# A transformer block with a mixture of experts: the experts' weights applied by one broadcast product on GpSimd instead of four multiplications on ScalarE

## The reference

```python
g_idx = argmax(g_logits)                        # one of 2 groups per token
topv, topi = top_k(softmax(e_sel), 2)           # 2 of the group's 4 experts
topv = topv / (topv.sum(-1) + 1e-8)
comb = zeros((S, 8)).at[rows, g_idx*4 + topi].add(topv)
h_expert = swiglu(flat @ expert_in_w.T)
for e in range(8):
    routed += comb[:, e:e+1] * (h_expert @ expert_out_weight[e].T)
out = out_shared + routed
```

## Time and profile before

| | |
|---|---|
| median of 3 runs | 1200.93 us (1200.56 to 1201.93) |
| span of the profiled execution, first to last instruction | 1198.4 us |
| time of the profiled execution with what lies around the span | not given by itself; median less span is 2.5 us |
| TensorE busy | 1062.6 us (89%) |
| VectorE busy | 760.6 us (63%) |
| ScalarE busy | 629.2 us (52%) |
| GpSimd busy | 388.1 us (32%) |
| mean granted TensorE clock | 0.939 of full speed |

### The profile page before, as it was taken

One profiled execution on the slowest core, in us unless ns is written; L12 is line 12 of the kernel. 1 busy time (PEld: TensorE's weight loads), 2 busy tenths in 40 slices (PEclk: granted clock), 3 DMA queues, 4 the chain that ended last, 5 costly groups with the idle time before them and its releaser, 6 DMA issues.

```text
span 1198.4 us, 20365 instructions
## 1 busy us (share of the span) xinstructions
PE 1062.6 (89%) x5632; PEld 707.3 (59%) x5632; DVE 760.6 (63%) x2118; ACT 629.2 (52%) x1395; POOL 388.1 (32%) x514
## 2 busy tenths in 40 slices
PE   2579988999799988899888998889989899899997
PEld 1345566556675566655666556755567455675575
DVE  3378547873768547686486854777467763778444
ACT  1226825567345745467344672546734576456744
POOL 5411424314341234313352142431433213341133
PEclk9969989999898998899889998989988999899999
DMA  3430033004040040400413003310314004040000
GB/s 94 71 40 2 14 41 59 19 2 54 10 59 10 1 53 10 67 1 1 53 26 50 1 11 42 55 22 1 41 12 66 13 2 53 10 63 1 1 2 18
DMA packets 28540, 34.39 MB, mean 29 GB/s; under 512 B 5402, under 2 KB 15552, under 8 KB 28336
## 3 DMA queue, kind: packets, MB, share of 16 engines
q1 hardware_dynamic: 28464, 33.55, 18.2%
HBM read 3.61 MB, written 4.19 MB: 7 GB/s over the span
## 4 chain that ended last, share of the span: by engine, by line
PE 62%; issue 11%; DVE 8%; DMA 6%; POOL 5%; SPq 4%; ACT 3%; DVEq 0%; POOLq 0%; ACTq 0%
PE bank L523 12%; PE pair L494 10%; PE bank L542 9%; PE bank L494 5%; DMA k_stack<-qk_h 5%; SPq L367 4%; PE pair L662 4%; PE pair L663 4%; PE pair L664 4%; PE bank L643 2%; ACT pt L975 2%; PE pair L425 1%; PE pair L426 1%; PE pair L427 1%; PE bank L644 1%
## 5 line engine op out<-in xcount | busy, mean ns | idle before, releaser
L975 ACT ACTIVATE pt<-bank 128x512 f32<-128x512 f32 (+3 forms) x768 | 348.6, 494 | 230.8 <-PE bank L523 223.6
L747 DVE CUSTOM_DVE_ANT_0 pair<-pair,causal 128x640 f32<-128x640 f32 (+3 forms) x256 | 258.8, 1046 | 59.3 <-PE pair L494 44.8
L523 PE MATMUL bank<-q_stack,k_stack 128*128 128x512 f32 (+2 forms) x768 | 268.9, 402 | 7.8 <-ACT pt L975 6.3
L523 PEld LDWEIGHTS bank<-q_stack,k_stack 128*128 128x128 f32 x768 | 137.9, 193 | 160.2 <-ACT pt L975 127.6
L1119 POOL TENSOR_SCALAR_AFFINE_SELECT pt<-pt 128x512 f32<-128x512 f32 x128 | 81.6, 638 | 391.9 <-ACT pt L975 391.9
L494 PE MATMUL pair<-k_stack,q_stack 112*128 112x512 f32 (+2 forms) x512 | 156.2, 396 | 22.6 <-DVE mx L747 12.3
L747 DVE CUSTOM_DVE_ANT_0 bank<-bank,causal 128x128 f32<-128x128 f32 (+3 forms) x256 | 122.6, 507 | 73.3 <-PE bank L494 73.1
L542 PE MATMUL bank<-pt,v 128*32 128x512 f32 (+3 forms) x1536 | 165.5, 503 | 2.2 <-POOL pt L1119 1.8
L494 PEld LDWEIGHTS pair<-k_stack,q_stack 112*128 112x128 f32 x512 | 90.9, 202 | 62.4 <-DVE mx L747 42.3
L494 PE MATMUL bank<-k_stack,q_stack 112*128 112x256 f32 (+2 forms) x256 | 90.0, 424 | 33.2 <-DMA k_stack<-qk_h 23.8
L662 PE MATMUL pair<-wex_h,hid_h 128*128 128x512 f32 x256 | 106.3, 415 | 0.7 <-POOL hid_l L1142 0.4
(11 more groups left out here) (142 smaller groups left out, 1528.7 us busy)
## 6 DMA issues: line engine op xcount, KB each, us to landing
q_stack<-qk_h SPq DMA_DIRECT2D x64, 128.0 KB, 4.1
k_stack<-qk_h SPq DMA_DIRECT2D x64, 128.0 KB, 6.2
q_stack<-qk_l SPq DMA_DIRECT2D x32, 128.0 KB, 5.0
k_stack<-qk_l SPq DMA_DIRECT2D x32, 128.0 KB, 6.7
out<-h SPq DMA_DIRECT2D x16, 256.0 KB, 2.3
pt<-w_expert SPq DMA_DIRECT2D x1, 1024.0 KB
x_sb<-x_t SPq DMA_DIRECT2D x8, 116.0 KB
pos_sb<-pos SPq DMA_DIRECT2D x1, 512.0 KB
```

Of the source, the lines that this page charges most:

```text
L523: nc.tensor.matmul((b4, b5)[p % 2][:, c0:HALF], k_stack[:, hd // 2, kt * P:(kt + 1) * P], q_stack[:, half, hd, c0:HALF], start=True, stop= ...
L747: nc.vector.tensor_tensor_reduce(src, src, causal[:, S - n:S], 1.0, -3.0e38, ALU.add, ALU.max, mx[:, col:col + 1]).then_inc(s_taken, 1)
L975: nc.scalar.activation(pt[:, k % PT_SLOTS, j, q0:HALF], (b4, b5)[p % 2][:, q0:HALF], ACT.Exp, scale=0.25).then_inc(exp_done, 1)
```

## The change

The four multiplications on ScalarE and their semaphore go. GpSimd waits for VectorE's `sel_made` itself and makes all four products with one `tensor_tensor` of 4 x 128 columns, in which `wsel` is broadcast along the 128 columns; it counts as a fourth step of `ex_step`, so every wait on `ex_step` counts by 4 per tile. The three additions stay.

```diff
-COMBINE = 3
+COMBINE = 4
...
-                elif kind == "combine":
-                    t = st[1]
-                    act.wait_ge(sel_made, i * TILES + t + 1)
-                    for e in range(EG):
-                        part = slice(e * P, (e + 1) * P)
-                        nc.scalar.mul(from_act[:, t % 2, part], from_dve[:, t % 2, part],
-                                      wsel[:, t, e:e + 1]).then_inc(weighted, 1)
...
-                pool.wait_ge(weighted, (i * TILES + t + 1) * EG)
+                pool.wait_ge(sel_made, i * TILES + t + 1)
+                nc.gpsimd.tensor_tensor(four.rearrange("p (e c) -> p e c", c=P),
+                                        from_dve[:, slot, :].rearrange("p (e c) -> p e c", c=P),
+                                        wsel[:, t, :].unsqueeze(2).to_broadcast([P, EG, P]),
+                                        ALU.mult).then_inc(ex_step, 1)
+                pool.wait_ge(ex_step, done + 1)
                 nc.gpsimd.tensor_tensor(two, four[:, 0:2 * P], four[:, 2 * P:4 * P], ALU.add).then_inc(ex_step, 1)
                 if t % HT == 0:
                     pool.wait_ge(base_made, i * 2 + t // HT + 1)
-                pool.wait_ge(ex_step, done + 1)
+                pool.wait_ge(ex_step, done + 2)
                 nc.gpsimd.tensor_tensor(acc[:, t, :], acc[:, t, :], two[:, 0:P], ALU.add).then_inc(ex_step, 1)
-                pool.wait_ge(ex_step, done + 2)
+                pool.wait_ge(ex_step, done + 3)
                 nc.gpsimd.tensor_tensor(acc[:, t, :], acc[:, t, :], two[:, P:2 * P], ALU.add).then_inc(ex_step, 1)
```

More of the change, by code:

```diff
@@ L300, in build @@
         shared_ready, base_made = sem("shared_ready"), sem("base_made")
-        ex_ready, sela_made, sel_made, weighted, ex_step = (
-            sem(n) for n in ("ex_ready", "sela_made", "sel_made", "weighted", "ex_step"))
+        ex_ready, sela_made, sel_made, ex_step = (sem(n) for n in ("ex_ready", "sela_made", "sel_made", "ex_step"))
         out_done = [sem(f"out_done_{half}") for half in range(2)]
@@ L1042, in stage @@
                     front(i, st[0], st[1])
-                elif st[0] in ("in", "counts", "expert", "combine"):
+                elif st[0] in ("in", "counts", "expert"):
                     forward(i, st)
```

## The result

The kernel with the change takes 1222.43 us (median of 4 runs, 1221.86 to 1225.06), the one before 1200.74 us (4 runs, 1200.00 to 1201.93): 1.0183 times as long, 95% interval 1.0169 to 1.0197.

A forecast was written before the change was run, and what follows sets the result against it. The prediction took the kernel as bound by TensorE and its waits, chiefly for VectorE's z. It summed 7 x 2.4 = 16.8, image 7 +1.7 and clock +1.4 to 19.9 us, giving 1220.5 us, range 1207 to 1230.

The forecast's parts named there:

- likeliest case: Whole kernel: products on GpSimd hold VectorE one instruction each; 1220.5 us, own range 1216 to 1225, chance 0.52.
- Removed products: ScalarE's 256 products, 81.7 us, go; what is queued behind them waits for other engines, so gain on the path 0.
- Price of the product: GpSimd's new 128x512 product taken at 1.29 us from the nearest row; a combine becomes 1.37 us longer.
- One VectorE instruction per GpSimd instruction: VectorE instructions with two SBUF inputs, and its z, are held; about one gets through per wide GpSimd instruction.
- The stage: Combines 2 and 3 of a steady image: routing and next z held, last z 2.4 us later, combine 1's 0.2 included.
- combine 1: Steady image: the combine ends at 605.0, not 604.18, and overlaps z2, which passes +0.2 us to TensorE's transposes.
- Combine 0 and combines 4 to 7: Rest of a steady image: products take as long as before, are hidden or end in time; cost 0.
- Image 7: Last image: product meets the routing, +0.4 us, and GpSimd runs without rest at the end, +1.3 us; 1.7 together.
- Clock: TensorE after the z stall: a longer stall makes the slow stretch more common, +0.2 us per image, 1.4 us.
- milder holding: Rival: only the instruction that meets a product waits longer, 1.4 us per image; 1212 us, chance 0.25.
- freed ScalarE: Rival: L899 of tile 1 waited for L1021 behind ScalarE's products, up to 1.27 us per image gained; 1191 us, chance 0.03.
- missing hold: Rival: no hold for a product reading few distinct weights, or VectorE wins the race; only the end longer, 1202 us, chance 0.08.

The follow-up runs named there:

- the kernel with six tiles on GpSimd: The changed kernel, but tiles 2 and 3 of each image keep ScalarE's four products: 1200.14 us, ratio 1.0010 to the kernel before.
- the gate: GpSimd starts combine 2 only when the next image's last z is made: 1193.29 us added to the kernel before, 1211.40 us added to the changed kernel.
- the changed kernel with the wait: The changed kernel, with GpSimd's combine 2 held back until the next image's last z is made: 1211.40 us, ratio 1.0073 to the kernel before.
- the eleven unused matmuls: Kernel before, combine 2 waiting for the last z, 5 unused matmuls in TensorE's stall, 11 more at an image's start: 1189.96 us, ratio 0.9938.
- the kernel before with the same wait: The kernel before, with GpSimd's combine 2 held back until the next image's last z is made: 1193.29 us, ratio 0.9941.

## Why the prediction was right

1220.5 us was forecast and 1222.43 measured, in the likeliest case's own range. The accounting below is of the profiled 21.7 us: TensorE's waits for z +12.0 and z2 +1.3; its smaller waits for VectorE +1.2 (L493 for mx 8.5 to 9.5, for from_dve 4.6 to 5.5, and so on, by the lists of both kernels); the same matmuls at a lower clock +6.0; from the last matmul to the last GpSimd start 4.59 us, before 4.11, +0.5. That is 21.0, of which 15.0 are the waits and the longer end; 0.7 us are not placed.

- **Removed products: gain 0.** Right. Loading ScalarE again changed nothing that can be measured; leaving the product out altogether gained 0.13%, which bounds what any freed engine could give.
- **Price of the product.** 1.29 us was taken, and "nothing suggests less" was wrong: 1.04 us. The Trainium skill's figure (GPSIMD Engine Reference, section 3.1; an estimate of 1.11 us by that page) was nearer than the nearest row, but by chance: with a full-width second operand the same product takes 1,284 ns. So the operand sets the price here, and not the width alone.
- **One VectorE instruction per GpSimd instruction.** Right, and it decided. The order differed in one place: L822 and L823 went through close together, next to the 0.07 us between the last two additions of combine 2, so that L825 was held by the last of them (0.43 us) and not by the second product. The four z met the second product and the three additions after it.
- **The stage: 2.4 us per image.** Measured 1.70 us, and 0.15 from combine 1 (from GpSimd's rs L1124 to z2t_l L1127, start to start 608.28 to 615.43 or 7.15 us, before 7.00): 1.85, so 13 us and not 16.8. The product's price is nearly all of the miss: with 1,284 ns the stage takes 2.15 us more than before, and with the 0.2 forecast for combine 1 that is 2.35.
- **Combine 0 and combines 4 to 7: 0.** Right within 0 to 2.4 us (the interval of the kernel with six tiles on GpSimd).
- **Image 7: 1.7 us.** Mis-sized too, by about 0.5 us: the z2 there rose from 2.40 to 2.73 us, and the end grew by 0.5 us, not 1.3. GpSimd without rest, as forecast, but at 2.9 us per combine and not 3.15.
- **Clock: 1.4 us.** The term that was too small: TensorE's busy time for the same matmuls rose by 6.0 us. The prediction charged the clock only behind the z stall. There it was right that a longer stall brings the lower level more often (transposes of 1.12 us in seven images of seven, before in three). But by windows of 3 us the grant falls to 0.50 in about four places of an image, at the turn of the loop and around the k_stack transfers too, and the places differ between the two traces. The misses of the stage and of image 7, together -4 to -5 us, and +4.6 here cancelled, and the smaller waits (+1.2) had no term at all. The median hit is partly luck, the sign and the mechanism are not.
- **Signs foretold.** L1142 at 1.04 (1.29 foretold), mean z 608 ns (800 or more), L812 0.91 us where the product meets it (1.2), TensorE's wait 46.1 us (about 50), combines at the end 2.9 us apart (3.1). All in the foretold direction, all smaller, by the product's price; for the mean z the 800 was also bad arithmetic, since the held stage has 28 of the 64 z: 7 x (2.99 - 1.57) is 9.9 us, all of the 10.0 by which the group grew (22.8 to 32.8 us).
- **Rivals.** The chances as listed add up to 0.89 for slower and 0.03 for faster, not 0.88 and 0.04. The milder holding (1212 us, +1.4 us per image) is closer in the stage's size than expected, 1.70 beside 1.4 and 2.4, but its reason is wrong: it had each product hold one instruction for its excess over an addition, which at the measured 1.04 us would be 0.9 us per image (L812 0.91 for 0.60, a z 1.04 for 0.46). The stage grew by 1.70 us for two products of 2.08 us together, and by another 0.45 when they became 2 x 0.24 us longer. The freed ScalarE and the missing hold fell with the experiments above.

Left open: the 0.7 us, and why the clock falls where it does. That the clock matters is shown for the changed kernel, where filling the stall gave 15 us. That it takes just 6.0 us in the change is read from busy times and not isolated: filling the stall of the kernel before gained only 2 us, though its mean grant rose from 0.939 to 0.954.

## What to carry to other kernels

Work moved from ScalarE to GpSimd is not free because GpSimd is idle: count the SBUF-to-SBUF instructions that VectorE has on the path meanwhile, one GpSimd instruction for each, and add the lengths of those that they meet. Judge a product by the engine that it holds up, tile by tile: here 48 of 64 could move for 0 to 2.4 us and 16 cost 20 us. When such a hold is removed by ordering, look at once for who stands behind the delayed work in the same queue or waits for its buffers; the gate that gained 7.9 us in one kernel gave back 17.6 of 24.3 us in the other.

## What the runs showed of the hardware

- A GpSimd product whose second operand has step 0 along its inner 128 columns takes 1,042 ns for 128x512; with a full operand 1,284, as with an operand broadcast along the outer dimension.
- VectorE instructions with two SBUF inputs, and its z, got through one per GpSimd instruction: 0.17 us for 4 columns with GpSimd still, 0.91 behind the product; 1.11 us for four z with GpSimd still, 1.57 across two additions, 2.99 across the product and three additions.
- The time of one and the same program goes with the clock it is granted. The runs of the changed kernel with the wait, in us and mean granted clock (from the list of its runs, not the profile):

```
1214.02 0.939   1201.89 0.951   1204.03 0.949   1214.09 0.941   1211.43 0.944
1202.88 0.949   1214.27 0.940   1211.38 0.943   1207.06 0.948   1211.68 0.944
```

  That is 12 us of spread for 0.012 of clock. The same stall does not always meet the same clock either: behind the 1.4 us stall for z the transposes took 1.11 us (the lower level) in four of the seven images and 0.66 in three, in this kernel and in the kernel before with the same wait alike. And a higher mean grant need not give time, as the eleven unused matmuls showed. So medians 1% apart, as here, need a look at the clock before a cause is named.
